# Attention over real keys, two heads stacked in 96 rows, and a routine of its own for three layer norms

## The chip, the cores and the metric

One NeuronCore of a Trainium2 chip runs the whole program in one launch. The metric is the device time in microseconds of that core; smaller is better. The engines are TensorE (PE; its weight loads are listed as PEld), VectorE (DVE), ScalarE (ACT), GpSimd (POOL) and SyncE (SP), which issues the DMA transfers. They run side by side and wait for one another only at semaphores.

## The reference

The model is a four-layer perceiver on 8 batches of 64 latent tokens with 256 features. Each layer has a cross attention, a self attention or recurrence, and a feed-forward part. Two places matter here. The first is the cross attention of the last layer (`l3x`), over a context of 1601 keys with 128 features per batch, with 16 heads of 16 features:

```
Q = (x @ Wq.T).reshape(B, xN, NUM_HEADS, HEAD_DIM)
KV = (z @ Wkv.T).reshape(B, zN, 2, NUM_HEADS, HEAD_DIM)
attn = jax.nn.softmax(jnp.einsum('bqhd,bkhd->bhqk', Q, K) * SCALE, axis=-1)
O = jnp.einsum('bhqk,bkhd->bqhd', attn, V).reshape(B, xN, DIM)
return O @ Wo.T
```

The second is the very start, where three layer norms stand behind one another before the first attention: the plain norm of `x`, `ln1` with gain and bias, and the norm that opens the attention (its result is kept once with the gain and bias `lnx`, once with `lny`).

## The kernel before

**Precision.** Operands of the large products are split in a high part (rounded to fp32r) and a low part (the rest). A product is then three matmuls, high by high, high by low and low by high; this is `three_passes`, lines 611 to 613 of the profile.

**Cross attention.** Three stages use `cross_attention`: the second attention of layer 0, `l2x` and `l3x`. The key projection is folded into the query: `queries` multiplies each head's query by that head's rows of Wk, so that q has 128 rows (the context's features) for each head, and the raw context (transposed, `cTh`, `cTl`) serves as keys for all heads. The work runs in units of two heads by 64 tokens, which are 128 rows. A batch has 8 units, the stage 64. Two units make a *couple*, u with slot 0 and u+1 with slot 1; there are 32 couples. For one unit v:

- PE computes the scores, 1602 columns in four tiles (290, 512, 512, 288) with three passes each, into PSUM banks 0 to 3, of which there is one set. The first two tiles make half 0, the others half 1.
- DVE takes the maximum of each half (L1066, L1068) and forms its negative (`ntop`, L1071).
- ACT takes the exponential of each half (L1010), into `normed` for slot 0 and `probs` for slot 1.
- PE transposes the 13 chunks of 128 keys in four groups g = 0 to 3 of 4, 4, 4 and 1 chunks (`turn_first` for slot 0, `turn_second` for slot 1, L921). ACT keeps the high part (`keep`, L1021), DVE the low part (`low`, L1079).
- For a couple, PE multiplies by the context, 13 chunks of three passes over 256 columns (`values(g, ...)`), and DVE stores the result (L1090).

Each engine has a fixed order of its own. DVE's in a couple is low(0) of unit v-1, maximum(v), low(1), low(2), low(3) of v-1, maximum(v+1), low(0), low(1) of v, store, low(2), low(3) of v. PE's is turn_second(0), scores(u), turn_second(1), turn_second(2), values(0), turn_second(3), values(1), scores(u+1), turn_first(0), turn_first(1), values(2), turn_first(2), values(3), turn_first(3). `values(1)` waits for low(1) of unit v-1:

```
pe.wait_ge(low_kept, 4 * (2 * c + 1) + g + 1)
```

SP fetches the next batch's context twice (transposed and by rows) into the one buffer `raw`. ACT rounds each of them (L1001), and POOL forms its low part (L863). POOL also splits the couple's q in `qh` and `ql` (`stage`, L870 and L875).

**Start.** `rows_to_norms` runs the three norms tile by tile (four tiles of 128 tokens), with unused transposes on PE between the real ones (`turn_unused`, L276). `statistics` of the context (DVE, L1901 to L1917) run beside the projections that follow.

Blocks (`nc.Block`) end with a barrier over the engines.

## Time and profile before

| | us |
|---|---|
| median of 3 runs | 2267.64 (2262.94 to 2269.9) |
| the profiled execution, its own time | 2266.19 |
| its span in the trace | 2264.4 |
| granted TensorE clock, mean | 0.955 |
| PE busy | 2049.1 (90%) |
| DVE busy | 1389.0 (61%) |
| ACT busy | 1131.4 (50%) |
| POOL busy | 507.4 (22%) |

The time of an execution lies 1.8 us above its span. The end of a matmul in the trace is modelled and overlaps the next one, so PE's rate is read from the distance between the starts of matmuls, not from their durations. The l3x attention runs from 1684.5 to 2078 us of the span.

### The profile page before, as it was taken

To read this page: it belongs to the slowest core of one execution; us is meant where nothing else is said; L and a number is where in the kernel's file an instruction comes from. 1 tells how busy PE (TensorE), PEld (TensorE's weight loads), DVE (VectorE), ACT (ScalarE), POOL (GpSimd) and SP (SyncE) were. 2 spreads that over 40 slices of the span, in tenths; PEclk is the share of its full clock that TensorE was granted. 3 is DMA by queue.
4 is the path that set the end of the run, shared out by engine and by line. 5 is a ranking of instruction groups with operands and counts; after the bars stand their busy time and mean duration, and the time that the engine had idled before them with its cause. 6 is when DMAs were issued, how large, how long until landed. Compare 5 with 4: busy or idle time off the path is not lost. (4 is left out here: it accounts for less than half of the span.)

```text
span 2264.4 us, 42645 instructions
## 1 busy us (share of the span) xinstructions
PE 2049.1 (90%) x15334; PEld 1775.2 (78%) x15334; DVE 1389.0 (61%) x2707; ACT 1131.4 (50%) x2279; POOL 507.4 (22%) x410
## 2 busy tenths in 40 slices
PE   5887999999887998489899999987979999999898
PEld 2765999999666875287799999966859999997687
DVE  7465777777455453721677777745447777775466
ACT  3245666666423432321566666624446666664254
POOL 2322222221012420101322222012332122220034
PEclk9798999999997998789999999999989999999999
DMA  5153101100141213531101100002220010000022
GB/s 214 37 237 118 45 31 32 44 30 0 36 149 58 99 34 138 214 146 56 45 31 36 40 30 30 0 17 72 75 93 32 31 43 32 30 15 0 19 79 77
DMA packets 32317, 144.06 MB, mean 64 GB/s; under 512 B 3632, under 2 KB 9136, under 8 KB 28848
## 3 DMA queue, kind: packets, MB, share of 16 engines
q1 hardware_dynamic: 32176, 142.23, 17.5%
q8 instruction: 83, 1.36, 0.2%
q14 instruction: 58, 0.48, 0.1%
HBM read 125.59 MB, written 13.90 MB: 62 GB/s over the span
## 5 line engine op out<-in xcount | busy, mean ns | idle before, releaser
L1021 ACT ACTIVATE pTh<-ps 128x512 fp32r<-128x512 f32 (+1 forms) x768 | 353.9, 519 | 384.2 <-PE ps L921 382.0
L1079 DVE TENSOR_TENSOR pTl<-ps,pTh 128x512 fp32r<-128x512 f32 (+1 forms) x768 | 416.0, 583 | 128.4 <-ACT pTh L1021 128.1
L611 PE MATMUL ps<-pTh,ch 128*128 128x256 f32 (+1 forms) x1248 | 383.5, 307 | 2.6 <-DVE pTl L1079 2.5
L612 PE MATMUL ps<-pTl,ch 128*128 128x256 f32 (+1 forms) x1248 | 348.4, 279 | 0.0
L613 PE MATMUL ps<-pTh,cl 128*128 128x256 f32 (+1 forms) x1248 | 348.0, 279 | 0.0
L611 PE MATMUL ps<-cTh,qh 128*128 128x512 f32 (+2 forms) x768 | 276.2, 360 | 20.7 <-POOL ql L875 13.5
L613 PE MATMUL ps<-cTh,ql 128*128 128x512 f32 (+2 forms) x768 | 268.8, 350 | 0.0
L612 PE MATMUL ps<-cTl,qh 128*128 128x512 f32 (+2 forms) x768 | 268.4, 349 | 0.0
L1066 DVE TENSOR_REDUCE top<-ps 128x1 f32<-128x802 f32 x192 | 189.4, 986 | 111.1 <-PE ps L613 111.1
L611 PEld LDWEIGHTS ps<-pTh,ch 128*128 128x128 f32 (+1 forms) x1248 | 235.1, 188 | 16.7 <-DVE pTl L1079 12.8
L612 PEld LDWEIGHTS ps<-pTl,ch 128*128 128x128 f32 (+1 forms) x1248 | 235.7, 189 | 0.0
L613 PEld LDWEIGHTS ps<-pTh,cl 128*128 128x128 f32 (+1 forms) x1248 | 234.6, 188 | 0.0
L1068 DVE TENSOR_REDUCE top<-ps 128x1 f32<-128x799 f32 x192 | 188.9, 984 | 13.8 <-PE ps L613 3.5
L1010 ACT ACTIVATE normed<-ps,ntop 128x802 f32<-128x802 f32 x192 | 176.9, 927 | 30.6 <-DVE ntop L1071 28.3
L921 PE MATMUL ps<-ident,probs 128*128 128x128 f32 (+1 forms) x1248 | 183.0, 273 | 3.9 <-DVE pTl L1079 2.4
L921 PE MATMUL ps<-ident,normed 128*128 128x128 f32 (+1 forms) x1248 | 183.7, 273 | 1.4 <-DVE pTl L1079 1.2
L611 PEld LDWEIGHTS ps<-cTh,qh 128*128 128x128 f32 x768 | 146.3, 190 | 41.6 <-POOL ql L875 16.3
L1010 ACT ACTIVATE probs<-ps,ntop 128x802 f32<-128x802 f32 x192 | 176.9, 937 | 0.0
L612 PEld LDWEIGHTS ps<-cTl,qh 128*128 128x128 f32 x768 | 147.2, 192 | 17.3
L613 PEld LDWEIGHTS ps<-cTh,ql 128*128 128x128 f32 x768 | 146.6, 191 | 16.9
L921 PEld LDWEIGHTS ps<-ident,probs 128*128 128x128 f32 (+1 forms) x1248 | 146.9, 140 | 5.8 <-ACT probs L1010 3.5
L921 PEld LDWEIGHTS ps<-ident,normed 128*128 128x128 f32 (+1 forms) x1248 | 147.2, 141 | 2.1 <-DVE pTl L1079 2.1
(349 smaller groups left out, 3645.1 us busy)
## 6 DMA issues: line engine op xcount, KB each, us to landing
w<-l1f_w_in SPq DMA_DIRECT2D x16, 1024.0 KB, 8.2
raw<-ctxT_in SPq DMA_DIRECT2D x16, 801.0 KB, 4.2
raw<-ctx_in SPq DMA_DIRECT2D x14, 832.0 KB, 4.5
wg<-l0f_guide_in SPq DMA_DIRECT2D x10, 704.0 KB, 5.1
z<-ctx_in SPq DMA_DIRECT2D x8, 832.0 KB, 12.8
z<-z SPq DMA_DIRECT2D x8, 832.0 KB, 10.8
keys<-ctx_in SPq DMA_DIRECT2D x8, 832.0 KB, 10.2
zT<-zT SPq DMA_DIRECT2D x8, 801.0 KB, 8.8
```

The lines of the kernel that those rows point to most:

```text
L611: pe.matmul(out, high, moving_high, start=start, stop=False)
L612: pe.matmul(out, high, moving_low, start=False, stop=False)
L613: return pe.matmul(out, low, moving_high, start=False, stop=stop)
L921: last = pe.transpose(ps[0:w, turned_bank[slot][g], k * P:(k + 1) * P], probs[slot][:, chunk * P:chunk * P + w], ident[:])
L1010: nc.scalar.activation(probs[slot][:, cols], flat[:, cols], ACT.Exp, bias=ntop[:, slot:slot + 1], scale=scale, accum_out=sums[:, bass.ds(2 ...
L1021: nc.scalar.activation(pTh[0:w, PARTS[g][0]:PARTS[g][0] + n, slot, :], ps[0:w, turned_bank[slot][g], 0:n * P].rearrange("p (k r) -> p k r" ...
L1066: dve.tensor_reduce(top[:, slot, 0:1], flat[:, half_cols[0]], AX.X, ALU.max).then_inc(top_step, 1)
L1068: dve.tensor_reduce(top[:, slot, 1:2], flat[:, half_cols[1]], AX.X, ALU.max)\
L1079: dve.tensor_tensor(pTl[0:w, at, slot, :], ps[0:w, turned_bank[slot][g], 0:n * P].rearrange("p (k r) -> p k r", r=P), pTh[0:w, at, slot, : ...
```

## The change

**Attention of l3x.** `many_head_cross("l3x", ...)` becomes `paired_head_cross`; the other two cross attentions stay as they are. The keys of all heads are now really projected (`project_keys`: 128 rows, that is 8 heads of 16 features, by about 400 columns, three passes), and the key's high part, its high part once more and its low part are copied by DMA below one another, in 96 rows: `stacked[96, 8, 1602]`, one slab for each pair of heads. The query tile `qs` holds high, low and high parts in the same 96 rows, with the other head's 16 rows masked to zero. One matmul with 96 rows then gives what three passes gave. Key tiles of the next batch are computed during this batch: two of about 400 columns in each couple (not in the last batch), kept by ACT (`keep_key`), split by POOL (`split_key`), and moved by SP in four halves of 12 transfers for each batch (`move_half`). The rounding of the raw context goes from ACT to POOL (`split_raw`). `cTh` and `cTl` are single buffers now. The weights of l3a are fetched after the attention and no longer at its start.

Before the attention, `paired_keys` makes the masked queries and the keys of batch 0, and moves them, 48 transfers in all.

**Start.** `first_norms` runs the moments of x for all four tiles first, then the second norm's moments for all, and only then what needs the weights; the unused transposes are gone, and DVE takes two of the four `yT` tiles from ACT.

```diff
+        def paired_attention(q, scale, keys, sums):
+            PER, UNITS = H // 2, H
+            STEPS, COUPLES = B // 2, H // 2
+            LEAD = 290
+            SPLIT = LEAD + BANK
...
+                probs = normed[:, 0:KEYS], rooms[:, 0:KEYS]
...
+                def key_tiles(i, at, final):
+                    return () if final and i else tuple((at // 2, 2 * (at % 2) + j, j) for j in range(2))
...
+                        def fetch_rows(b):
+                            sp.wait_ge(low_ready, 2 * b - 1)
+                            sp.dma_start(raw[:], dram["ctx"][bass.ds(b, 1)].rearrange("b p k -> (b p) k"))\
+                                .then_inc(raw_landed, 16)
+                        def fetch_keysT(b):
+                            sp.wait_ge(low_ready, 2 * b - 2)
+                            sp.dma_start(raw[:, 0:KEVEN], dram["ctxT"][bass.ds(b, 1)].rearrange("b p k -> (b p) k"))\
+                                .then_inc(raw_landed, 16)
+                        def move(b, at):
+                            sp.wait_ge(key_low, 8 * b + 2 * at + 2)
+                            sp.sem_inc(move_seen, 1)
+                            if at % 2 == 0:
+                                sp.wait_ge(scores_ready, 8 * b + 4 + 2 * at)
+                            move_half(sp, keys, key_highs, key_lows, at // 2, at % 2, moved[at % 2])
+                        def batch(b, final=False):
+                            fetch_rows(b + 1)
+                            move(b, 0)
+                            move(b, 1)
+                            if not final:
+                                fetch_keysT(b + 2)
+                            move(b, 2)
+                            move(b, 3)
...
+                            pool.tensor_copy(qs[:, k % 2].rearrange("p (h s) -> p h s", s=S), q[0:STACK, heads, at])\
+                                .then_inc(high_staged, 1)
+                            pool.wait_ge(high_staged, c + 1)
+                            pool.sem_inc(high_seen, 1)
+                            pool.tensor_tensor(qs[32:64, k % 2].rearrange("p (h s) -> p h s", s=S), q[32:64, heads, at],
+                                               qs[32:64, k % 2].bitcast(F32).rearrange("p (h s) -> p h s", s=S),
+                                               ALU.subtract).then_inc(staged, 1)
...
+                                if not (final and k == COUPLES - 1):
+                                    stage(c + 1, 2 * step + (k + 1) // 4, (k + 1) % COUPLES, first and k < 1)
+                                if first and k == 0:
+                                    split_raw(1, keys.cTh[:], keys.cTl[:])
+                                for chunk, tile, j in key_tiles(i, at, final):
+                                    split_key(8 * b + 2 * at + j, tile)
+                                if at == 1 and not (final and i):
+                                    if first and i == 0:
+                                        pool.wait_ge(keys.first_moved[1], 2 * MOVES)
+                                    else:
+                                        pool.wait_ge(value_ready, 4 * b)
+                                    split_raw(2 * b + 2, ch[:, 1 - i], cl[:, 1 - i])
+                                if at == 3 and not final:
+                                    split_raw(2 * b + 3, keys.cTh[:], keys.cTl[:])
...
+                                last = pe.matmul(flat[:, score_cols[n]], qs[:, k, at:at + P],
+                                                 keys.stacked[:, u % PER, score_cols[n]], start=True, stop=True)
...
+                        def key_tile(u, step, j, final):
+                            i, at = u // PER, (u // 2) % 4
+                            for chunk, tile, n in key_tiles(i, at, final):
+                                if n == j:
+                                    if at == 0 and j == 0:
+                                        pe.wait_ge(low_ready, 2 * (2 * step + i) + 1)
+                                    if j == 1:
+                                        pe.wait_ge(key_kept, 8 * (2 * step + i) + 2 * at + 1)
+                                    project_keys(pe, keys, chunk, tile, 7).then_inc(key_ready, 1)
...
+                                pe.wait_ge(probs_half, v)
+                                turn_second(0, v - 1)
+                                scores(u, step, first)
+                                if first and u == 2:
+                                    key_bank_free(0, step, final)
+                                turn_second(1, v - 1)
+                                turn_second(2, v - 1)
+                                values(0, c - 1, i, first and u == 2, new_batch)
+                                turn_second(3, v - 1)
+                                if key_tiles(u // PER, (u // 2) % 4, final):
+                                    pe.wait_ge(low_kept, 4 * v - 2)
+                                key_tile(u, step, 0, final)
+                                values(1, c - 1, i)
+                                scores(u + 1, step, first)
+                                key_tile(u, step, 1, final)
+                                turn_first(0, v)
+                                turn_first(1, v)
+                                values(2, c - 1, i)
+                                key_bank_free(u, step, final)
+                                turn_first(2, v)
+                                values(3, c - 1, i)
+                                turn_first(3, v)
...
+                                    keep(3, v - 1, 1)
+                                    for chunk, tile, j in tiles:
+                                        keep_key(step, first, i, at, tile, j)
+                                keep(0, v, 0, c if before else None)
+                                keep(1, v, 0, c if before else None)
+                                exponents(v + 1, 1, first and u < 2, 0)
...
+                        for c in range(KC):
+                            last = pe.transpose(ps[:, t, c * P:(c + 1) * P], xn[:, t, c * P:(c + 1) * P], ident[:])
+                        last.then_inc(again_ready, 1)
...
+                    for n in range(2 * NT):
+                        deviation(act, n % NT, n + 1, var_ready, std_ready)
+                    weights_landed(act, "a1")
+                    deviation(act, 0, 2 * NT + 1, var_ready, std_ready)
+                    for t in range(NT):
+                        if t + 1 < NT:
+                            deviation(act, t + 1, 2 * NT + t + 2, var_ready, std_ready)
+                        keep_turned(act, t, 4 + t, [(xT, w("lnx_g"), w("lnx_b"))], turned_ready)
+                        if t + 2 < NT:
+                            keep_turned(act, t, t, [(yT, w("lny_g"), w("lny_b"))], again_ready)
...
+                    for t in range(NT):
+                        moments(t, x)
+                    for t in range(NT):
+                        inverse(t, t + 1)
+                        link(scaled(t, x))
+                        moments(t, xn)
+                    weights_landed(dve, "a1")
+                    gained(0)
+                    for t in range(1, NT):
+                        gained(t)
+                        last_norm(t - 1)
+                    last_norm(NT - 1)
...
-                    rows_to_norms([], [(x, xn, (), None), (xn, inner, (), (w("ln1_g"), w("ln1_b"))), (inner, xn, (), None)],
-                                  [(xT, w("lnx_g"), w("lnx_b")), (yT, w("lny_g"), w("lny_b"))],
-                                  landed=lambda engine: weights_landed(engine, "a1"))
+                    first_norms(w, yT)
...
+        K_COLS = [slice(0, 402), slice(402, 802), slice(802, 1202), slice(1202, KEVEN)]
+        K_HALVES = slice(0, 802), slice(802, KEVEN)
+        STACK = 3 * 32
+        MOVES = 16 * 12
...
+            cols = K_HALVES[half]
+            for j in range(4):
+                rows = slice(32 * j, 32 * j + 32)
+                for n, src in enumerate((high, high, low)):
+                    sp.dma_start(keys.stacked[32 * n:32 * n + 32, 4 * chunk + j, cols].bitcast(F32), src[rows, cols].bitcast(F32)).then_inc(moved, 16)
...
+                order_ = [("q", p) for p in range(4)] + [("k", 0, n) for n in range(4)] + \
+                         [("q", p) for p in range(4, 8)] + [("k", 1, n) for n in range(4)]
...
+                            sp.dma_start(raw[:, 0:KEVEN], dram["ctxT"][0]).then_inc(keysT_landed, 16)
+                            sp.dma_start(first_rows[:], dram["ctx"][0]).then_inc(rows_landed, 16)
+                            for chunk in range(2):
+                                for half in range(2):
+                                    sp.wait_ge(split_low, 2 + 4 * chunk + 2 * half + 2)
+                                    move_half(sp, keys, fetched[chunk][1], fetched[chunk][0].bitcast(F32R), chunk, half,
+                                              keys.first_moved[chunk])
...
+                            split(1, w("wk"), wkh[:], wkl[:])
+                            pool.wait_ge(keysT_landed, 16)
+                            split(2, raw[:, 0:KEVEN], cTh[:], cTl[:])
+                            for n, (what, *which) in enumerate(order_):
+                                if what == "k":
+                                    chunk, tile = which
+                                    src, high = (t[:, K_COLS[tile]] for t in fetched[chunk])
+                                    pool.wait_ge(taken[n % 2], n // 2 + 1)
+                                    split(3 + 4 * chunk + tile, src, high, src.bitcast(F32R))
...
+                with paired_keys(w, q) as keys:
+                    paired_attention(q, (D // H) ** -0.5, keys, places.sums)
+                fetch_next("l3x")
...
-        many_head_cross("l3x", HP, (D // H) ** -0.5, False)
+        paired_head_cross()
```

How the instructions stand on PE inside one couple, between the last chunk of turn_second (65 rows) and turn_first, in the kernel before. `cTh` and `cTl` are the context's high and low part, `qh` and `ql` the query's, `pTh` the transposed exponentials, `ch` the context by rows:

```order
L921 MATMUL ps<-ident,probs 65x128
L946 REGISTER_ALU
L611 MATMUL ps<-pTh,ch 128x256
...
L909 REGISTER_ALU
L611 MATMUL ps<-cTh,qh 128x290
L612 MATMUL ps<-cTl,qh 128x290
L613 MATMUL ps<-cTh,ql 128x290
L611 MATMUL ps<-cTh,qh 128x512
...
L921 MATMUL ps<-ident,normed 128x128 x8
```

The same place in the changed kernel. `wkh` and `wkl` are the parts of the key weights, `rooms` holds the exponentials of slot 1:

```order
L1312 MATMUL ps<-ident,rooms 65x128
L1375 ISA
L614 MATMUL ps<-cTh,wkh 128x400
L615 MATMUL ps<-cTl,wkh 128x400
L616 MATMUL ps<-cTh,wkl 128x400
L1339 REGISTER_ALU
L614 MATMUL ps<-pTh,ch 128x256
...
L1285 MATMUL ps<-stacked,qs 128x290
L1285 MATMUL ps<-stacked,qs 128x512 x2
L1285 MATMUL ps<-stacked,qs 128x288
```

A key tile has come ahead of values(1), and the twelve score matmuls behind it have become four; a second key tile follows the scores.

What SP issues from the start of l3x into its attention, before (`first_keys` takes the context by rows; the last row stands in the loop over batches):

```order
L785 DMA raw<-ctxT_in 128x1602
L788 DMA first_keys<-ctx_in 128x1664
L147 DMA weights_1<-l3a_in 128x3338
L54 ISA x6
L847 UNCONDITIONAL_BRANCH
L785 DMA raw<-ctxT_in 128x1602
```

And in the changed kernel (`weights_1`, `ch` and `second_low` are the rooms in which the key's parts lie before the move):

```order
L2626 DMA weights_1<-ctxT_in 128x1602
L2627 DMA first_rows<-ctx_in 128x1664
L2564 DMA stacked<-weights_1 32x802 x12
L2564 DMA stacked<-weights_1 32x800 x12
L2564 DMA stacked<-ch 32x802 x2
...
L2564 DMA stacked<-second_low 32x800
L2623 UNCONDITIONAL_BRANCH
```

Forty-eight small transfers now stand between the first fetch and the end of the block that comes before the attention.

## Rows read from the trace of the kernel before

**Rows 1.** Window 1700 to 2060: L1066 and its waits; windows: start:end, us, busy PE, PEld, DVE, ACT, POOL, clock.

```profile
L1066 DVE TENSOR_REDUCE top<-ps x59: 979/993/995, 1704.3 to 2055.0; 128x1 f32<-128x802 f32 x59
...
  PE ps L613: 30.0, 30
...
1696.40:2066.00 369.60, 367.55 (x2720) 346.54 (x2719) 269.32 (x459) 239.57 (x505) 78.59 (x71) 1.00 0.09 30
```

**Rows 2.** Timeline of one couple: start, duration, engine, operation, idle before.

```profile
2055.02 0.99 DVE L1066 TENSOR_REDUCE top<-ps 128x1 f32<-128x802 f32 x1 [1.03 <-PE ps L613]
...
2057.53 0.94 ACT L1010 ACTIVATE probs<-ps,ntop 128x802 f32<-128x802 f32 x1
...
2059.98 1.48 DVE L1079 TENSOR_TENSOR pTl<-ps,pTh 128x512 fp32r<-128x512 f32 x3 [0.25 <-ACT pTh L1021]
...
2061.39 0.98 DVE L1066 TENSOR_REDUCE top<-ps 128x1 f32<-128x802 f32 x1
...
2064.16 0.38 PE L611 MATMUL ps<-pTh,ch 128*128 128x256 f32 x1
...
2065.68 0.30 PE L611 MATMUL ps<-cTh,qh 128*128 128x290 f32 x1
...
2066.97 0.99 DVE L1066 TENSOR_REDUCE top<-ps 128x1 f32<-128x802 f32 x1 [1.02 <-PE ps L613]
```

**Rows 3.** Timeline, two score matmuls of 512 columns behind one another.

```profile
2066.31 0.39 PE L612 MATMUL ps<-cTl,qh 128*128 128x512 f32 x1
2066.54 0.40 PE L613 MATMUL ps<-cTh,ql 128*128 128x512 f32 x1
```

**Rows 4.** Timeline from the start of l3x to its second couple.

```profile
1667.15 0.33 SPq L785 DMA_DIRECT2D raw<-ctxT_in  x1
...
1671.35 1.52 POOL L792 CAST cTh<-raw 128x1602 fp32r<-128x1602 f32 x1 [5.64 <-DMA raw<-ctxT_in]
...
1672.95 3.56 POOL L794 TENSOR_TENSOR cTl<-raw,cTh 128x1602 fp32r<-128x1602 f32 x1
...
1684.52 0.40 PE L611 MATMUL ps<-cTh,qh 128*128 128x290 f32 x1 [2.86 <-POOL ql L875]
...
1696.37 0.38 PE L611 MATMUL ps<-cTh,qh 128*128 128x290 f32 x1
```

**Rows 5.** POOL's operations on 256 columns, window 1700 to 2060: ns min/median/max.

```profile
L870 POOL CAST qh<-q x29: 390/398/412, 1705.4 to 2044.2; 128x256 fp32r x16, 128x256 fp32r<-128x256 f32 x13
L875 POOL TENSOR_TENSOR ql<-q,qh x29: 729/739/745, 1706.0 to 2044.8; 128x256 fp32r<-128x256 f32 x29
```

**Rows 6.** DMA issues (KB each, us to landing), and issues on SP.

```profile
wd<-l3f_down_in SPq DMA_DIRECT2D x22, 128.0 KB, 2.1
...
v<-v SPq DMA_DIRECT2D x2, 512.0 KB, 5.9
...
5.41 3.76 SPq L1894 DMA_DIRECT2D z<-ctx_in  x8
...
58.69 0.72 SPq L530 DMA_DIRECT2D v<-v  x1
```

**Rows 7.** Timeline of the first norms and of what follows.

```profile
5.25 0.43 DVE L346 BATCH_NORM_STATS2 stat<-x 128x6 f32<-128x256 f32 x1 [5.25 <-PEq L167]
...
5.81 0.40 DVE L346 BATCH_NORM_STATS2 stat<-x 128x6 f32<-128x256 f32 x1
...
11.27 0.13 DVE L353 RECIPROCAL rstd<-std 128x1 f32<-128x1 f32 x1
...
12.45 0.13 DVE L353 RECIPROCAL rstd<-std 128x1 f32<-128x1 f32 x1
...
14.21 0.39 DVE L346 BATCH_NORM_STATS2 stat<-x 128x6 f32<-128x256 f32 x1
...
27.18 0.85 ACT L294 ACTIVATE yT<-ps,weights 128x128 f32<-128x128 f32 x2
...
57.83 0.40 DVE L1917 RECIPROCAL rdev<-dev 128x39 f32<-128x39 f32 x1 [0.30 <-ACT dev L1936]
```

More of the change, by code:

```diff
@@ L99 @@
 ContextKeys = namedtuple("ContextKeys", "cTh cTl ch cl raw fetch_keysT fetch_keys")
+HeadKeys = namedtuple("HeadKeys", "stacked raw cTh cTl ch cl wkh wkl qs high low first_moved first_rows low_ready")
 ContextNormaliser = namedtuple("ContextNormaliser", "fetch statistics deviations first_rows second_rows "
@@ L115, in perceiver_kernel @@
         x = sb("x", [P, NT, D])
-        inner = sb("inner", [P, NT, D])
-        mid = sb("mid", [P, NT, D])
+        rooms = sb("rooms", [P, 2 * NT * D])
+        inner, mid = (rooms[:, n * NT * D:(n + 1) * NT * D].rearrange("p (t d) -> p t d", t=NT) for n in range(2))
         normed = sb("normed", [P, NT * D + KC * N])
@@ L1125, in share_places @@
+        def share_places(dh, where, sums=None, inverse=None):
+            if sums is None:
+                sums = sb("sums", [P, B * H], where=where)
+                inverse = sb("inverse", [P, B, 32], where=where)
             heads = sb("heads", [2 * 32, H * dh], F32R, where)
@@ new lines, in paired_head_cross @@
+        def paired_head_cross():
+            weights_here("l3x")
+            w = weights("l3x")
+            per = H * HP // P
+            with ExitStack() as tmp:
+                q = sb("q", [P, H, N], where=tmp)
+                places = share_places(HP, tmp, rooms[:, KEVEN:KEVEN + B * H],
+                                      rooms[:, KEVEN + B * H:KEVEN + B * H + B * 32].rearrange("p (b j) -> p b j", b=B))
+                with paired_keys(w, q) as keys:
+                    paired_attention(q, (D // H) ** -0.5, keys, places.sums)
+                fetch_next("l3x")
+                oT = sb("oT", [P, per, N], where=tmp)
+                late_values(w("wv"), q, oT, HP, places)
@@ L2685 @@
     arrays = {n: np.ascontiguousarray(v) for n, v in arrays.items()}
-    nc = bacc.Bacc("TRN2", target_bir_lowering=False, num_devices=1)
+    nc = bacc.Bacc("TRN2", target_bir_lowering=False, num_devices=1, dynamic_dma_scratch_size=2048)
     dram = {n: nc.dram_tensor(n + "_in", v.shape, mybir.dt.from_np(v.dtype), kind="ExternalInput").ap()
```

396 lines of the change are left out of this document (389 added, 7 removed).

## The prediction

> **What bounds the kernel now.** I read the page first, which gives PE 90% of the span, and then looked at l3x alone, since the change acts on three places only: the first norms, the block before the l3x attention, and that attention. In the attention the window over 30 couples shows PE busy 367.6 of 369.6 us at clock 1.00, DVE 269 and ACT 240 [rows 1]. A couple takes 369.6/30 = 12.3 us with two stray stalls in it; the undisturbed ones lie at 12.0. That looks like a plain PE bound. The timeline of one couple shows that it is also something else. The maximum of a unit (L1066) starts at 2055.02, 2061.39 and 2066.97, that is 6.37 and 5.58 us apart [rows 2], and before every other one DVE has waited 1.0 us for PE's last score matmul, 30.0 us in 30 waits [rows 1]. So PE, DVE and ACT go round in one loop in which nobody has slack: making PE's part cheaper shortens the couple only where the shortened work stands in that loop. I therefore follow two links.
>
> Link 1, 5.58 us: maximum at 2061.39, its second half and `ntop`, low(1) done at 2064.1, values(1) start 2064.16, scores(u+1) start 2065.68, maximum 2066.97 [rows 2]. Link 2, 6.37 us: maximum at 2055.02, exponentials from 2057.53, the transposes and ACT's copies, the lows at 2059.98, and the next maximum behind low(0) at 2061.39 [rows 2]; here DVE's own order and ACT's copies count, and PE hardly waits.
>
> **The first norms: −4.5 us.** The block's work ends with ACT at 27.18 + 0.85 = 28.0 [rows 7]. In the new order the moments of x take 4 × 0.56 (the distance 5.25 to 5.81), from 5.25 to 7.5, and the second norm's 4 × 1.18 (11.27 to 12.45), to 12.2. Only then are the weights wanted, which now hold DVE up until 10.7. The part with gains costs 14.21 − 12.45 = 1.76 for the first tile, and (1.76 + 0.49) for each of three more: 20.7. The last norm's tail, a transpose and one copy add 2.8, so the block ends at about 23.5, not 28.0: −4.5. The removed transposes kept PE awake, and the projections that follow may start at the lower clock level; but their block ends with DVE's statistics at 58 [rows 7], so I cost that at nothing. If PE were the last there, it would cost some 2 us.
>
> **The block before the attention: +22.7 us.** Before, the raw fetch goes out at 1667.15, lands at 1671.35, POOL casts for 1.52 and subtracts for 3.56, and the first scores start at 1684.52 [rows 4]. Now nothing can be projected before cTl is there (1676.5). The first key tile (three passes of 402 columns, then ACT's copy) is out at about 1678.3. POOL splits it: interpolated over columns between 0.40 and 1.52 us for the cast and 0.73 and 3.56 us for the subtraction [rows 4, 5], 402 columns take 0.52 + 1.0, with 0.18 between them 1.7 us. Two tiles are ready at 1681.8, and SP starts to move. It has 48 transfers to issue. Issues behind one another take 3.76/8 = 0.47 us [rows 6]; with 0.48, 23.0 us: the last goes out at 1704.8 and lands 2.1 to 2.5 us later, as small transfers do [rows 6]. First scores at 1707.2 against 1684.5: +22.7. Bounds: a lone issue shows 0.33 [rows 4], which gives 1681.8 + 15.8 + 2.3 = 1699.9, +15.4; one from SBUF to SBUF shows 0.72 [rows 6], which gives 1718.7, +34. I take 0.48, since eight rows in a run are the same thing. No engine has other work to cover this: the whole of PE waits, and starts the attention at a lower clock, some tenths of a us.
>
> **The first couple: +1.8 us.** It took 1696.37 − 1684.52 = 11.85 [rows 4]. Both its key tiles now stand behind low(2) and behind one another through one bank: two times about 0.55 on PE, an ACT copy of 0.5 between them and waits. I take 13.7.
>
> **27 couples with key tiles: −8.6 us.** PE's work falls. A score pass of 512 columns costs 0.23 us, the distance of two starts [rows 3]; 1602 columns three times over are 2.2 us a unit, of which two thirds go: −2.92 for a couple. Two key tiles of 400 columns bring 6 × 0.183 = +1.10. PE then needs 12.0 − 1.8 = 10.2 us, and no longer sets the couple's length. What does is the loop.
> Link 1: scores half 0 fall from 1.10 to 0.37 (−0.73), but key tile 0 stands before values(1) and waits for the same low(1) as it, and so its 0.55 goes into the link whole: 5.58 − 0.73 + 0.55 = 5.41.
> Link 2: the second half's scores are ready 0.7 us sooner, which DVE can't use, as its maximum of half 0 takes 0.98 anyway. The transposes behind come forward by 0.9, but key tile 1 (0.55) and ACT's copies of both key tiles (0.5 each) come in ahead of ACT's copies of the exponentials. Of 6.37 I leave 6.23.
> Together 11.64 against 11.96: −0.32 for each of 27. I know the second link worst: were ACT's copies fully in it, nothing is gained; were they fully covered, −0.6. So 0 to −16.
>
> **The last 4 couples, without key tiles: −4.6.** Link 1 gains the whole 0.73, link 2 0.4.
>
> **Costed at nothing, with their cover.** The raw roundings leave ACT (1.6 us each, twice a batch), which has 35% idle. POOL takes them: it was busy 79 of 370 us [rows 1], and now splits two key tiles a couple (3.4 us), the query (1.1) and twice a batch 1602 columns (5.1). Its tightest place is the first key tile of a batch, which PE wants 14.4 us after the batch's start, against a cTl ready at 13.3 to 13.9. SP's moves in the loop: the first starts 17.3 us after a batch's start, 12 issues of 0.48 and 2.3 for the landing make it 25.4, and ACT wants the room again at 27.7. The l3a weights, fetched after the attention, are wanted over 20 us later.
>
> The sum, against the profiled execution's own 2266.2: −4.5 + 22.7 + 1.8 − 8.6 − 4.6 = +6.8, so 2273.0. This execution lies 1.4 under the median of the runs, 2267.64. I say 2274. About 0.3% (7 us) is what a measurement of this kernel can tell from no change.
>
> **Rivals.**
> *PE is the bound after all*, and the order of DVE and ACT gives way, so that a couple shrinks by PE's own saving. PE at 367.6 of 369.6 speaks for it; against it, that DVE waits for PE at one place only, 1.0 us a couple, so no couple can shrink by more unless link 2 shrinks too. The time: 2266.2 − 4.5 + 22.7 + 1.8 − 27 × 1.83 − 4 × 2.92 = 2225. It decides as soon as a couple saves over 0.75 us. Faster; chance 0.17.
> *The moves are bound by their bytes, not by their issue.* Each reads and writes only 32 partitions. 512 KB from SBUF to SBUF land in 5.9 us, 128 KB in 2.1 [rows 6]; taken as 3.8 us for the 512 KB that is 138 GB/s. A half (12 × 32 × 802 × 4 B = 1.23 MB) then takes 8.9 us, four of them and the two fetches of context (4.4 each) 44.4 of a batch's 46.6 us, and ACT's copy of a key tile waits in most batches: 14 × 0.9 = +12.6; the start costs another 12.6. 2274 + 25 = 2299. Against it speaks that the v transfers may be slow for their own form, and that the price is worked out from two sizes only. Chance 0.14.
> The Trainium skill has a rule on this (SBUF — State Buffer, Door 1: the DMA port swizzle): transfers on 32 partitions and on 64 reach the same 8 of 16 ports, and partitions 0 to 31 alone were measured at 189 GB/s at 1 MiB. By it a half would take 6.5 us, the start about 3 us longer than by issues, and the loop would hide the rest. No row here shows 32-partition transfers.
> *POOL comes too late with cTl.* Its margin is 0.5 us; if its subtraction takes longer beside DVE, PE waits up to 1 us in each of 7 batches: 2274 + 7 = 2281. Chance 0.11.
>
> **How the numbers follow.** The main case has 0.58, with its own range 2258 to 2291: from 2274 the couples' −8/+8 and the start's −7/+11, added as if independent, with some us for the rest. The range over all cases, 2245 to 2303, reaches part of the way to the first rival and past the second; about 1 in 10 is left below and less above. Slower by over 0.3% (above 2274.5): half of the main case, all of the second rival and most of the third, with part of the main case's upper half: 0.48. Within 0.3% 0.26; faster 0.26, the first rival and the main case's lower end.
>
> **What would show it.** Right: SP issues 48 transfers 0.48 us apart before the attention, and the first scores are 22 us later in the block than before; the maxima lie 5.4 and 6.2 us apart; PE shows about 1 us idle in each couple, put down to low(1); the first block ends near 24; the last batch's couples last 10.8. Wrong: couples of 10.5 us or less with PE busy throughout, or with waits of PE for `moved` at the start of batches, or moves that land over 6 us after their issue.

## The result, and the profile after

| | before | after |
|---|---|---|
| median of 9 runs each, us | 2270.42 | 2281.0 |
| ratio, 95% interval | | 1.0056 (1.0038 to 1.0074) |
| the profiled execution, its own time | 2266.19 | 2289.7 |
| its span | 2264.4 | 2287.9 |
| granted TensorE clock, mean | 0.955 | 0.943 |

The change makes the kernel slower, by 12.7 us (8.6 to 16.8) by the ratio and 10.6 by the medians. The forecast was 2274 in a range of 2245 to 2303, with "slower by over 0.3%" as the likeliest sign at 0.48.

The two profiled executions lie 23.5 us apart, twice as far as the medians. Their traces can be laid beside one another by the starts of DMA transfers that both have:

| stretch | before | after | difference |
|---|---|---|---|
| start to first v transfer | 58.69 | 54.52 | −4.2 |
| from there to the l3x raw fetch, without the next row | 1561.8 | 1567.1 | +5.3 |
| self-attention of layer 0: its first v transfer to the l1x weights | 46.7 | 53.6 | +6.9 |
| l3x: raw fetch to late_values (`rl`) | 415.55 | 433.52 | +18.0 |
| `rl` to the end | 181.7 | 179.2 | −2.5 |

The rows that carry this are these. The timeline of the changed kernel from the start of l3x to the first scores, which answers to [rows 4]:

```profile
1675.21 0.33 SPq L2626 DMA_DIRECT2D weights<-ctxT_in  x1
...
1679.64 1.52 POOL L2637 CAST cTh<-weights 128x1602 fp32r<-128x1602 f32 x1 [4.72 <-DMA weights<-ctxT_in]
...
1684.32 0.45 PE L614 MATMUL ps<-cTh,wkh 128*128 128x402 f32 x1 [2.42 <-POOL cTl L2639]
...
1688.70 1.87 SPq L2564 DMA_DIRECT2D stacked<-weights  x3
...
1718.62 0.59 SPq L2564 DMA_DIRECT2D stacked<-second_low  x1
...
1719.87 0.39 POOL L1222 CAST qs<-q 96x256 fp32r<-96x256 f32 x1 [17.04 <-POOLq L2623]
...
1721.31 1.00 PE L1285 MATMUL ps<-stacked,qs 96*128 96x290 f32 x2 [25.45 <-POOL qs L1226]
```

The reader is to see that PE, which still projects key tiles while the first moves go out, sits idle for the 25.45 us from 1695.9 to the first scores, and that the moves fill this time. The first scores come 46.1 us after the raw fetch; in [rows 4] it was 1684.52 − 1667.15 = 17.4. That is +28.7. Of the 46.1 us 29.9 lie between the first issue of a move (1688.70) and the last (1718.62), 0.637 us from one of the 48 to the next; a single one is recorded with 0.59. The row of the first scores names POOL's query tile `qs` as what released them: POOL begins it at 1719.87, once the block with the moves has ended. The last move lands 2.2 us behind its issue, at about 1720.8, so its landing would have held PE nearly as long.

The maxima of consecutive units in the changed kernel, DVE's timeline in a couple, for [rows 2]:

```profile
1749.47 0.98 DVE L1473 TENSOR_REDUCE top<-ps 128x1 f32<-128x802 f32 x1
...
1754.89 0.99 DVE L1473 TENSOR_REDUCE top<-ps 128x1 f32<-128x802 f32 x1 [0.86 <-PE ps L1285]
...
1761.08 0.98 DVE L1473 TENSOR_REDUCE top<-ps 128x1 f32<-128x802 f32 x1
...
1766.52 0.99 DVE L1473 TENSOR_REDUCE top<-ps 128x1 f32<-128x802 f32 x1 [0.88 <-PE ps L1285]
```

They lie 5.42, 6.19 and 5.44 us apart, a couple 11.63, against 11.96 before. PE at the key tile, and the busy time of the engines over 230 us of the attention:

```profile
1752.24 0.45 PE L614 MATMUL ps<-cTh,wkh 128*128 128x402 f32 x1 [0.77 <-DVE pTl L1486]
```

```profile
1760.00:1990.00 230.00, 206.53 (x1535) 191.46 (x1534) 170.19 (x293) 156.99 (x351) 119.82 (x134) 0.99 0.55 141
```

PE was busy for 367.6 of 369.6 us before [rows 1]. Now it is busy for 206.5 of 230 us and idle in each couple, 0.77 us ahead of the key tile in this row, until DVE's `pTl` (low(1)) is there. All its waits in that stretch:

```profile
PE ps L614 <- DVE pTl L1486: 16.9, 20, 1.5
PE ps L1312 <- DVE pTl L1486: 6.5, 20, 0.4
```

POOL is busy 120 of 230 us, as it takes over splits, and the DMA share went from 0.09 [rows 1] to 0.55. No wait of PE for `moved` and none for POOL stands in the list. The first block: DVE's last work in it is the two `yT` tiles, and the next block's statistics start at 24.37, where they started at 28.53.

```profile
21.84 1.58 DVE L2264 TENSOR_SCALAR yT<-ps,weights 128x128 f32<-128x128 f32 x4 [0.38 <-PE ps L2205]
...
24.37 5.12 DVE L2376 BATCH_NORM_STATS2 stats<-z 128x6 f32<-128x128 f32 x26 [0.94 <-PEq L2199]
```

### The profile page after: what moved, and what is told of

The parts are those of the page before. It is cut to its first block and busy times, and to the rows that moved or that the text cites. A ratio compares the mean times of both kernels' runs of the same rounds, so it can differ in the third digit from the quotient of the medians.

```text
span 2287.9 us, 42847 instructions
## 1 busy us (share of the span) xinstructions
PE 2016.2 (88%) x14978; PEld 1734.5 (76%) x14978; DVE 1390.2 (61%) x2714; ACT 1139.0 (50%) x2320; POOL 609.4 (27%) x552
## 5 line engine op out<-in xcount | busy, mean ns | idle before, releaser
L614 PEld LDWEIGHTS ps<-pTh,ch 128*128 128x128 f32 (+1 forms) x1248 | 236.1, 189 | 16.5 <-DVE pTl L1082 8.2
L614 PE MATMUL ps<-cTh,qh 128*128 128x512 f32 (+2 forms) x512 | 185.1, 362 | 16.0 <-POOL ql L878 11.2
L616 PE MATMUL ps<-cTh,ql 128*128 128x512 f32 (+2 forms) x512 | 179.9, 351 | 0.0
L615 PE MATMUL ps<-cTl,qh 128*128 128x512 f32 (+2 forms) x512 | 179.7, 351 | 0.0
L1069 DVE TENSOR_REDUCE top<-ps 128x1 f32<-128x802 f32 x128 | 126.3, 986 | 76.1 <-PE ps L616 76.1
L1071 DVE TENSOR_REDUCE top<-ps 128x1 f32<-128x799 f32 x128 | 125.9, 984 | 10.0 <-PE ps L616 3.2
L1013 ACT ACTIVATE normed<-ps,ntop 128x802 f32<-128x802 f32 (+1 forms) x128 | 117.9, 927 | 20.5 <-DVE ntop L1074 19.0
L924 PE MATMUL ps<-ident,normed 128*128 128x128 f32 (+1 forms) x832 | 122.5, 273 | 1.0 <-DVE pTl L1082 1.0
L614 PEld LDWEIGHTS ps<-cTh,qh 128*128 128x128 f32 x512 | 98.1, 192 | 29.9 <-POOL ql L878 12.9
L1013 ACT ACTIVATE probs<-ps,ntop 128x802 f32<-128x802 f32 (+1 forms) x128 | 118.0, 937 | 0.0
L614 PE MATMUL ps<-xh,wgh 128*128 128x512 f32 (+1 forms) x280 | 112.8, 403 | 5.1 <-DVE gated L1937 3.7
L615 PE MATMUL ps<-xl,wgh 128*128 128x512 f32 (+1 forms) x280 | 112.3, 401 | 0.0
```

The costliest lines, as they stand in the source:

```text
L614: pe.matmul(out, high, moving_high, start=start, stop=False)
L615: pe.matmul(out, high, moving_low, start=False, stop=False)
L616: return pe.matmul(out, low, moving_high, start=False, stop=stop)
L924: last = pe.transpose(ps[0:w, turned_bank[slot][g], k * P:(k + 1) * P], probs[slot][:, chunk * P:chunk * P + w], ident[:])
L1013: nc.scalar.activation(probs[slot][:, cols], flat[:, cols], ACT.Exp, bias=ntop[:, slot:slot + 1], scale=scale, accum_out=sums[:, bass.ds(2 ...
L1069: dve.tensor_reduce(top[:, slot, 0:1], flat[:, half_cols[0]], AX.X, ALU.max).then_inc(top_step, 1)
```

## The experiments

All ratios are to the kernel before, run on the same chip as the version named. "Scores" is the time from the l3x raw fetch to the first scores of the version's profiled execution, "l3x" that from the same fetch to `rl`. In the edits below, unchanged lines and repeated arguments are shortened.

| version | median, us | ratio (95%) | scores | l3x | maxima apart |
|---|---|---|---|---|---|
| after | 2281.0 | 1.0056 (1.0038 to 1.0074) | 46.1 | 433.5 | 5.43 and 6.19 |
| early_key | 2279.4 | 1.0025 (1.0009 to 1.0041) | 46.1 | 422.5 | 4.95 and 6.18 |
| pe_extra | 2284.4, one run | | 46.1 | 434.6 | 5.44 and 6.18 |
| whole_rows | 2285.5 | 1.0059 (1.0042 to 1.0076) | 41.4 | 429.9 | 5.44 and 6.18 |
| issue_forms | 2298.6, one run | | 51.9, longer by design | 440.2 | 5.44 and 6.18 |
| norms_only | 2276.3 | 1.0015 (0.9991 to 1.0039) | 17.5 | 414.8 | as before |
| two_queues | 2273.3 | 1.0010 (0.9989 to 1.0032) | 40.1 | 425.9 | 5.42 and 6.18 |
| two_whole | 2283.7 | 1.0048 (1.0023 to 1.0072) | 40.3 | 428.2 | 5.44 and 6.18 |
| two_early | 2270.0 | 0.9991 (0.9970 to 1.0012) | 39 | 412.8 | 4.95 and 6.18 |
| old_norms | 2289.2 | 1.0080 (1.0066 to 1.0095) | 46.1 | 434.5 | 5.44 and 6.18 |
| dve_order | 2273.4 | 1.0020 (1.0001 to 1.0039) | 39 | 424.1 | 5.08 and 6.38 |
| two_early_old | 2271.0 | 1.0006 (0.9987 to 1.0025) | 39 | 413.4 | 4.95 and 6.18 |
| before_again | 2274.6, one run | | 17.5 | 415.4 | as before |

The l3x column orders the versions more finely than the ratios do. The profile of the kernel before gives 415.6 there and a second one of it (before_again) 415.4, while the ratios also carry what differs elsewhere: whole_rows is 3.6 us shorter than the changed kernel in l3x, and its ratio is no lower.

**What a couple's length hangs on: early_key and pe_extra.**

```
-  turned_bank = (4, 5, 7, 4), (5, 7, 4, 5)
+  turned_bank = (4, 5, 7, 4), (5, 7, 4, 7)
...
+  key_tile(u, step, 0, final)          # bank 5, free after low(0)
   turn_second(3, v - 1)
-  pe.wait_ge(low_kept, 4 * v - 2)
-  key_tile(u, step, 0, final)
   values(1, c - 1, i)
   scores(u + 1, step, first)
+  pe.wait_ge(low_kept, 4 * v)
   key_tile(u, step, 1, final)          # bank 7
```

> The changed kernel with its first key tile of a couple in the PSUM bank that low(0) frees (5, no longer 7), put ahead of turn_second(3), and turn_second(3) in bank 7. In the changed kernel PE idles about 0.8 us a couple ahead of that tile, waiting for low(1), and the maxima lie 5.43 and 6.2 us apart; in the last batch, which has no key tiles, 4.89 and 6.02. Theory (the couple is a loop through DVE, ACT and PE, and the tile costs its 0.55 us only because it stands behind low(1)): the tile slides into the idle time, 5.43 becomes 4.9, the 6.2 stays, each of 27 couples loses 0.5 us, the run is 12 to 15 us faster than the changed kernel. Rival (PE's amount of work sets the couple): the work is the same, so no change.

The other one fills the pause with work that is thrown away:

```
+  for _ in range(7):
+      pe.transpose(ps[0:w, turned_bank[1][3], 0:P], probs[1][:, last chunk], ident[:])
   turn_second(3, v - 1)
   pe.wait_ge(low_kept, 4 * v - 2)
   key_tile(u, step, 0, final)
```

> The changed kernel with seven more transposes of the last chunk (about 0.1 us each, 0.7 us in all) ahead of turn_second(3), so in the time in which PE idles for low(1). They write what turn_second(3) writes again behind them. Theory (loop): the maxima stay 5.43 and 6.2 us apart, and only PE's idle time ahead of the key tile shrinks from 0.8 to about 0.1 us. Rival (PE's work sets the couple): every couple grows by 0.7 us, 19 us in all.

DVE's timeline in early_key:

```profile
1761.59 0.98 DVE L1473 TENSOR_REDUCE top<-ps 128x1 f32<-128x802 f32 x1
...
1766.53 0.99 DVE L1473 TENSOR_REDUCE top<-ps 128x1 f32<-128x802 f32 x1 [0.37 <-PE ps L1285]
...
1772.71 0.98 DVE L1473 TENSOR_REDUCE top<-ps 128x1 f32<-128x802 f32 x1
```

4.94 and 6.18 us. PE's waits in 1760 to 1990, first of early_key:

```profile
PE ps L1312 <- DVE pTl L1486: 13.1, 39, 0.4
PE ps L614 <- DVE pTl L1486: 1.8, 1, 1.8
```

and of pe_extra:

```profile
PE ps L1312 <- DVE pTl L1492: 6.5, 20, 0.4
PE ps L614 <- DVE pTl L1492: 1.9, 1, 1.9
```

The same matmuls in another order took 0.49 us off a couple; from the first maximum to `rl` it is 375.3 against 386.4 us, 11.1 less (12.5 gained in the couples with key tiles, 1.4 lost behind them). In the whole time early_key lies 0.31% ± 0.24 under the changed kernel, that is 7 us (2 to 12), where 12 to 15 had been expected. Seven more transposes a couple cost nothing: the 16.9 us of waiting ahead of the key tile shrank to 1.9, and the maxima stayed 5.44 and 6.18 apart. So the changed kernel's couple is not set by how much PE does, and the first rival, in which a couple shrinks by all that PE saves, is out: PE's work fell by some 1.8 us a couple, as worked out in the prediction, the couple by 0.33. Of the kernel before this is not shown. No run changed PE's work alone there, and with PE 99.4% busy it may have been bound by PE, with the loop's limit 0.33 us behind.

**What the start hangs on: whole_rows, issue_forms, two_queues, two_whole.** In whole_rows each transfer takes all 1602 columns, and 24 do the work of 48:

```
- for half in range(2):
-     sp.wait_ge(split_low, 2 + 4 * chunk + 2 * half + 2)
-     move_half(..., chunk, half, keys.first_moved[chunk])
+ sp.wait_ge(split_low, 2 + 4 * chunk + 4)
+ move_half(..., chunk, whole row, keys.first_moved[chunk])
```

> The changed kernel, with the moves ahead of the attention in whole rows: 24 transfers of 32 x 1602 in place of 48 of about 32 x 801. Each waits for all four tiles of its half of the heads, so the first goes out about 3 us later. Theory (what counts is the number of issues, 0.64 us each): the block loses 24 x 0.64 = 15.3 us and gains 3, first scores about 12 us earlier after the raw fetch than the changed kernel's 46.1 us, so 34. Rival (bytes, or the rows described, bound the queue): transfers lie 1.28 us apart, and the scores come 3 us later, at 49.

The DMA view of the moves in the changed kernel (1660 to 1720), issue time in ns, least/median/most:

```profile
L2564 SPq DMA_DIRECT2D stacked<-weights x24: 589/592/598, 1688.7 to 1703.3; - x24
...
DMA to landing us min/median/max: 2.2/2.2/2.2
```

and of whole_rows (1680 to 1718), with its window over the moves:

```profile
L2564 SPq DMA_DIRECT2D stacked<-weights x12: 589/932/1010, 1691.9 to 1701.5; - x12
...
DMA to landing us min/median/max: 2.9/4.1/4.3
```

```profile
1692.00:1714.00 22.00, 4.22 (x17) 2.71 (x15) 4.91 (x6) 3.93 (x5) 7.69 (x8) 0.70 0.95 205
```

Neither expectation came out. The scores came 4.7 us sooner, not 12. The shortest issue in this row is still 589 ns, but the median is 932, a landing takes 4.1 us and no longer 2.2, and the DMA engines are busy 95% of the time at 205 GB/s. In the changed kernel they were busy 67% of it, at 157 GB/s:

```profile
1689.00:1719.00 30.00, 6.86 (x23) 3.69 (x21) 6.28 (x7) 4.91 (x7) 10.08 (x12) 0.69 0.67 157
```

With halves the issues were the limit (all within 589 to 599 ns, every landing 2.2 us), with whole rows it is the bytes. The two limits are close: 48 × 0.637 = 30.6 us by issues, 4.92 MB at 205 GB/s = 24.0 us by bytes.

issue_forms puts eight transfers of other forms behind the 48, on the same queue: four from HBM to 32 rows of 802 elements, four of 128 rows of 200 from SBUF to SBUF.

```
+ sp.dma_start(raw[32 * n:32 * n + 32, 0:802], dram["ctxT"][0][32 * n:32 * n + 32, 0:802])   # four
+ sp.dma_start(raw[:, 802 + 200 * n:1002 + 200 * n], first_rows[:, 200 * n:200 * n + 200])   # four
```

> The changed kernel with eight more transfers behind the 48 moves ahead of the attention, only to see how far apart their issues lie: four of 32 x 802 from HBM, and four of 128 x 200 from SBUF to SBUF. Moves lie 0.64 us apart, fetches from HBM to 128 rows lay 0.47. Theory A (a source in SBUF makes the issue dearer): 0.47 for the four from HBM, 0.64 for the four with 128 rows. Theory B (a form of 32 rows makes it dearer): 0.64 for the first four, 0.47 for the others. The run itself is some 6 to 8 us longer.

SP's timeline there:

```profile
1720.94 0.60 SPq L2564 DMA_DIRECT2D stacked<-second_low  x1
1721.59 1.97 SPq L2635 DMA_DIRECT2D weights<-ctxT_in  x4
1723.60 2.46 SPq L2638 DMA_DIRECT2D weights<-first_rows  x4
```

(1723.60 − 1721.59)/4 = 0.50 us for each that comes from HBM, 2.46/4 = 0.62 for each that comes from SBUF, in a row with moves at 0.64. Theory A holds: the source makes the difference, not the number of rows. The run's l3x part is 6.7 us longer than the changed kernel's, within the 6 to 8 expected; as a whole this one run is 17.6 us above the changed kernel's median.

two_queues gives the second half of the heads to ACT's queue and projects all key tiles ahead of the last queries; two_whole does so with whole rows.

```
  @block.scalar
      act.activation(ch[:, 0], first_rows[:], ACT.Copy)
+     for half in range(2):
+         act.wait_ge(split_low, 6 + 2 * half + 2)
+         move_half(act, keys, fetched[1][1], fetched[1][0], 1, half, keys.first_moved[1])
```

> The changed kernel, with the second half of the heads moved by ACT's queue ahead of the attention (24 transfers on SP, 24 on ACT), and all key tiles projected ahead of the last four query tiles so that ACT's transfers can start at about 20.7 us after the raw fetch. Theory of issues: each queue goes at 0.64 us a transfer, SP ends at 28.8, ACT at 36, and the scores start at about 38.5 us after the raw fetch, in place of 46.1. Rival, bytes: the run with whole rows moved 205 GB/s with the DMA engines 95% busy; 4.92 MB at that rate take 24 us, from 13.5 to 37.5, and where both queues run the issues lie further apart than 0.64. Scores then at 40 to 41.

> The same with whole rows, 12 transfers of 32 x 1602 on each queue. Issues alone would end it at about 16.5 + 7.7 = 24 on SP and 20.7 + 7.7 = 28.5 on ACT, scores at 31. By bytes, 4.92 MB at 205 GB/s from 16.5 on: done at 40.5, scores at 41 to 42. If two queues move more than one did, because their transfers touch different partitions, something between.

ACT's queue in two_queues, while SP's is running too, and the window of two_whole over its moves:

```profile
1700.16 2.09 ACTq L2564 DMA_DIRECT2D stacked<-ch  x2
1702.28 0.63 ACTq L2564 DMA_DIRECT2D stacked<-second_low  x1
1702.93 1.75 ACTq L2564 DMA_DIRECT2D stacked<-ch  x2
```

```profile
1686.00:1709.00 23.00, 4.44 (x11) 1.45 (x9) 5.09 (x5) 4.97 (x6) 8.31 (x13) 0.69 0.96 219
```

In two_whole two queues bring 219 GB/s over the window where one brought 205, the DMA engines busy 96%; behind SP's last issue, with the rest of its transfers and ACT's under way, it is more (the DMA share of 1.04 tells that so short a window is good to a few per cent only):

```profile
1697.00:1704.00 7.00, 0.00 (x0) 0.00 (x0) 0.00 (x0) 0.00 (x0) 0.00 (x0) 0.50 1.04 249
```

The last issue ended at 1704.5, yet PE waited for its landing until 1709.8, so here the bytes are the limit. The scores come 40.3 us after the fetch, between the 31 by issues and the 41 to 42 by bytes. In two_queues they come at 40.1, the number of the rival that reckons by bytes. But its end is set by issues: SP's are done at 1707.1, ACT's go on alone to 1714.3, every 0.64 us, with the DMA engines 74% busy in 1708 to 1714. No arrangement tried brought the scores below 39 us, and 17.4 was the kernel before. That 39 is the floor is not shown: at 249 GB/s the 4.92 MB would take 19.8 us (an estimate), and no version had both queues busy from the first move on.

**The two together: two_early, and dve_order.** two_early has the edits of early_key and two_queues.

> The edits of early_key and two_queues together. The parts add if they are independent: 14 us from the couples and 5 to 8 us from the block ahead of the attention, so 19 to 22 us faster than the changed kernel and 6 to 9 us (0.3 to 0.4%) faster than the kernel before. Rival: ACT, which now issues 24 transfers, holds up the end of its block or the attention's start, and only the 14 us are left: about level with the kernel before.

The l3x part took 412.8 us (2090.59 − 1677.76), 2.7 less than the kernel before and 20.7 less than the changed kernel, where 19 to 22 were expected. The ratio of 0.9991 (0.9970 to 1.0012) can't be told from no change, nor from the 1.0006 of two_early_old; 6 to 9 us under the kernel before were expected, 2 were measured (7 less to 3 more). By l3x it is the shortest version found: the projected keys, placed better, about pay for their start. Part of even the 2.7 us has another source. The 32nd and the 33rd maximum lie 8.23 us apart in the kernel before and 8.09 in the changed one, where their neighbours lie 6.5 and 6.3 apart. In two_queues, two_early, two_early_old and dve_order this pause of 1.8 us is missing. What makes it is not known; without it 0.9 us of the 2.7 is left. dve_order goes on from there:

```
  def maximum(v, slot, between):
      dve.tensor_reduce(top, half 0 of the scores)
+     low(1, v - 1, 1)
      dve.tensor_reduce(top, half 1 of the scores)
```

> two_early with one more edit: DVE takes low(1) of the unit before between the two halves of the maximum of slot 0. In early_key PE still idles 0.3 us a couple for low(1), and the maxima lie 4.95 and 6.2 us apart. Theory (the loop): low(1) comes 1.0 us sooner and the link behind it shortens until PE's own work is what is left (10.2 us a couple by the sum of its matmuls): couples of about 10.4 to 10.6 us in place of 11.15, 15 to 20 us less in all, and PE busy without a pause. Rival: the maximum's second half, 0.64 us later, delays the exponentials by as much, and the other link grows by what this one loses: couples stay at 11.1.

Its timeline on DVE:

```profile
1766.51 0.98 DVE L1473 TENSOR_REDUCE top<-ps 128x1 f32<-128x802 f32 x1
1767.41 0.68 DVE L1488 TENSOR_TENSOR pTl<-ps,pTh 128x512 fp32r<-128x512 f32 x1
...
1771.39 0.29 DVE L1488 TENSOR_TENSOR pTl<-ps,pTh 65x128 fp32r<-65x128 f32 x1 [1.55 <-ACT pTh L1431]
1771.60 0.98 DVE L1473 TENSOR_REDUCE top<-ps 128x1 f32<-128x802 f32 x1
```

It went the rival's way, and further: 5.08 and 6.38 us, a couple 0.33 longer than in two_early. low(3) waits for ACT's copy, which stands behind both exponentials, and these now start 0.6 us later. The next maximum stands behind low(3) on DVE and follows it at once, with no wait for PE. The wait on PE has become one on ACT.

**The first norms: norms_only, old_norms, two_early_old, before_again.** The first has the new routine alone, the second and third are the changed kernel and two_early with the norms of before, the last is the kernel before once more.

```
- rows_to_norms([], [(x, xn, (), None), (xn, inner, (), (w("ln1_g"), w("ln1_b"))), (inner, xn, (), None)], ...)
+ first_norms(w, yT)
```

> The kernel before with the new routine for the first three norms alone. Expected from the prediction's steps: the first block and the projections behind it end 4.2 us earlier (the first v transfer at 54.5, not 58.7, as in the changed kernel), and nothing else changes, so the run is 0.2% faster. Rival: the removed transposes let the TensorE clock fall in a later stage and the 4 us are given back; then the first v transfer stands at 54.5, but a stage behind it is longer.

> The changed kernel with the first norms of the kernel before: the attention's part of the change alone. From its trace the l3x part costs 18.0 us (46.1 instead of 17.4 us from the raw fetch to the first scores, 10.8 us back in the couples). If the norms gain 4.2 us that last to the end, this run is 4 us slower than the changed kernel, ratio 1.008 to the kernel before. If they are given back in later stages, as norms_only (1.0015) suggests, it is level with the changed kernel or faster, ratio 1.004 to 1.006, and the self-attention of layer 0 (46.7 or 53 to 55 us from its first v transfer to the next weights, in the runs so far) shows the short time.

> two_early with the first norms of the kernel before. By its trace two_early's l3x part takes 412.8 us from the raw fetch to late_values, against 415.6 in the kernel before and 434.5 in old_norms, so this one is 2.7 us under the kernel before, ratio 0.999, and 21 to 22 us under old_norms (1.008). If the new norms' 4.2 us last to the end, it is 4 us slower than two_early (0.9991), at 1.001; if they are given back by later stages it is level with it.

> The kernel before, unchanged, for a second profile of it: whether its self-attention of layer 0 (46.7 us from its first v transfer to the next weights) is also found at 53 to 55 us, as in six of nine profiles with the new norms. If it is a coin toss, either is likely; if the new norms bring it, 46.7 again.

old_norms measures the attention's part alone: +0.80%, 18.2 us (15.0 to 21.6), and its trace gives 434.5 us for l3x against 415.55, +19.0. The norms gain 4.1 us at their place in every profile (first v transfer at 54.5 to 55.2, in four profiles with the old norms at 58.5 to 58.7). In the whole time three pairs tell: norms_only +0.15% ± 0.24, after against old_norms −0.24% ± 0.23, two_early against two_early_old −0.15% ± 0.28. norms_only was expected 0.2% faster, and its interval (0.9991 to 1.0039) leaves out the full 0.18%. Weighted together the three give −0.08% ± 0.14, in which neither nothing nor the full 0.18% is excluded.

The gain shrinks on its way. The raw fetch of the next attention stands at 172.0 to 175.5 us with the new norms, 173.4 on average over ten profiles, and at 175.6 to 177.0 with the old, 176.1 over four: 2.7 of the 4.1 are left. At the first v transfer of the self-attention of layer 0 it is 662.2 (660.7 to 664.3) against 663.7 (663.2 to 664.8): 1.5 are left. Behind that this self-attention differs between executions. Its windows, before and after, at the same place of the program:

```profile
675.00:690.00 15.00, 12.26 (x308) 10.71 (x309) 7.25 (x19) 5.70 (x14) 3.20 (x2) 1.00 0.01 4
```

```profile
674.00:694.00 20.00, 17.37 (x301) 15.39 (x300) 5.45 (x12) 6.45 (x14) 1.36 (x1) 0.52 0.01 3
```

Some 300 matmuls, mostly of the same lines, at a granted clock of 1.00 in one and 0.52 in the other. Just ahead of it (663 to 670, and 662 to 670) the clock was 0.56 in the first and 0.97 in the second, so in the short execution the clock was low ahead of these matmuls and not during them. The stage takes 46.7, 50.1 or 53.6 to 55.0 us. With the new norms it was 53.6 or more in seven of ten profiles and 46.7 in three; with the old ones 46.7 twice and 50.1 twice. before_again, which was to tell 46.7 from 53 to 55, is one of the 50.1, and differs from the first profile of the same kernel by 3.4 us. Whether the norms bring the long form on, or chance does, stays open: fourteen profiles are too few. The stretch from `rl` to the end is no steadier: 181.7 and 186.7 us in the two profiles of the kernel before, 184.5 in old_norms, 179.2 in the changed kernel.

## Why the prediction was right or wrong

By its own steps, all from traces:

| step | predicted | measured |
|---|---|---|
| first norms | −4.5 | −4.2 at their place |
| block before the attention | +22.7 (bounds +15.4, +34) | +28.7 |
| first couple | +1.8 (between first scores) | +2.7 (15.50 from its first maximum to the next couple's, before 12.76) |
| 27 couples with key tiles | −8.6, 0.32 each | 0.33 each |
| maxima apart | 5.41 and 6.23 | 5.43 and 6.19 to 6.28 |
| last 4 couples | −1.15 each, 10.8 long | −1.05 each, 10.91 long |

The sign, the mechanism and the place of each term of l3x were right; the size of the largest was not. The l3x part was forecast at +11.3 and came out at +18.0. The term that was mis-sized is the issue of a move: 0.48 us was taken "since eight rows in a run are the same thing". They were not: those came from HBM, the moves come from SBUF, and issue_forms shows 0.50 for the one and 0.62 to 0.64 for the other. From the first issue to the last it took 29.9 us where 23.0 were forecast, 6.9 more. That the moves started 1.2 us sooner than forecast (13.5 after the fetch, 14.7 forecast) gave some back, and from the last issue to the scores it took 2.7 us, not 2.4, so the term is off by 6.0. The row that would have told was in [rows 6], the v transfer at 58.69, and served as the upper bound only. The first couple added another 0.9 us: PE ran it at a granted clock of 0.50 up to 1730, after 25 us without work, where the kernel before had 0.78 to 1.00 in its first couple. What part of the 0.9 is the clock's no run separates.

The total was forecast at +6.8 us and came out at +12.7 by the ratio, nearly twice as much. It lies inside the stated range because that range allowed for such a start: 11 us more for it in the main case alone.

That the loop and not PE's amount of work sets the changed kernel's couple is shown by early_key and pe_extra, and by the pause of 0.8 us that was forecast as 1 us. That key tile 0 costs its 0.55 us only by its place is shown by early_key, which moved it and its bank and gained 0.49. That the moves in the loop are hidden is shown by the changed kernel's waits, where in 1740 to 2070 none of PE's or ACT's is for them, though they too were issued every 0.66 us, and a batch's 48 take 32 of its 46.6 us. The cover is thin: in early_key, with its shorter couples, ACT waited for a move once, for 0.2 us. Of the rivals, PE as the bound is out. POOL too late with cTl is out: in 1740 to 2070 PE waits for DVE alone. The byte-bound moves are out for the changed kernel (landings of 2.2 us ahead of the attention, and 2.2 in the median, 3.6 at most, in 1750 to 2050), but the limit that this rival named is real and near: whole_rows and two_whole ran into it, at 205 to 249 GB/s, above the 138 that was worked out from the v rows. (That figure divides 512 KB by 3.8 us, the difference between the landings of 512 and of 128 KB; the 384 KB between them would give 103.) The Trainium skill (SBUF — State Buffer, Door 1: the DMA port swizzle) gives some 218 GB/s as what transfers on partitions 0 to 31, which reach 8 of 16 ports, approach. The 249 of two_whole lies above that figure, and its transfers are not of that kind alone: together they write partitions 0 to 95 and read 0 to 127. Whether the ports set the limit here is not shown, since no run tried the same bytes over other partitions.

The first norms were costed at −4.5 with nothing given back. At their place that is right. That nothing is given back was wrong as far as the profiles reach: 1.5 of the 4.1 us are left at 662. How much reaches the end is not settled.

Of the 23.5 us between the profiled executions, 6.9 lie in the self-attention of layer 0 and go with the clock. The comparison of many runs, not that of two traces, gives the change's size: 18.0 for l3x less what the norms keep, between the 1.5 left at 662 and the 4.2 at their place, makes 13.8 to 16.5; the ratio gives 12.7 (8.6 to 16.8).

## What to carry to other kernels

How busy an engine is does not tell what its saving will bring: follow the waits through one turn of the loop, since the next limit may lie just behind. Here 1.8 us less work for an engine that was 99.4% busy shortened the couple by 0.33. The same work placed in a pause is free, and placed behind the wait that ends the pause it costs nearly its full length: moving one key tile of 0.55 us brought 0.49 more. Count the small transfers that nothing covers, price them by a row with the same source and destination, and work out their bytes beside it, since the second limit may lie just behind the first.

## What the runs showed of the hardware

A transfer from SBUF to SBUF was issued every 0.62 to 0.64 us, one from HBM every 0.47 to 0.50, on the same queue. Transfers of 103 KB from SBUF to SBUF kept to the issue rate and landed in 2.2 us; of 205 KB they lay 0.91 us apart and landed in 4.1. One queue moved 205 GB/s of the latter (whole_rows, 1692 to 1714), two queues 219 over the whole of their window and 249 in 1697 to 1704 (two_whole). One self-attention ran its matmuls at a granted clock of 1.00 or 0.52 in different executions and took 46.7 or up to 55.0 us, while nothing in its own code had changed; in two executions of one and the same kernel it took 46.7 and 50.1.
